# Edge counts in a long one-core kernel: eight edge columns to one 16-bit compare, counted at a step of eight

## The reference, cut to what matters

```
src = jnp.concatenate([edge_index[0], loops])
dst = jnp.concatenate([edge_index[1], loops])
...
denom = jax.ops.segment_sum(ee, dst, num_segments=M)
msg = h[src] * alpha[:, :, None]
agg = jax.ops.segment_sum(msg, dst, num_segments=M).reshape(M, HEADS * NUM_EXPERTS) + b_gat
```

## Time and profile before

| | us |
|---|---|
| median of 3 runs | 13,044.54 (13,042.87 to 13,053.62) |
| profiled execution, its own time | 12,933.95 |
| span of the profile | 12,931.9 |
| PE busy in the span | 6,153.1 |
| DVE busy | 4,820.6 |
| POOL busy | 5,593.1 |
| ACT busy | 2,055.4 |
| L203 and L204, DVE, both stages | 2,253.1 |
| L211, PE, both stages | 598.7 |

### The profile page before, as it was taken

How to read it: one execution, slowest core, us unless ns; L and a number is a source line. 1 busy time by engine, 2 the same in 40 slices (tenths; PEclk the granted TensorE clock), 3 DMA queues, 4 the chain that set the end, 5 groups by cost and what they waited for, 6 DMA issues and landing times. The chain is left out here.

```text
span 12931.9 us, 89860 instructions
## 1 busy us (share of the span) xinstructions
PE 6153.1 (48%) x22715; PEld 3706.2 (29%) x22715; DVE 4820.6 (37%) x13519; ACT 2055.4 (16%) x3797; POOL 5593.1 (43%) x5292
## 2 busy tenths in 40 slices
PE   0115888988869967787322222222222222222256
PEld 0114666666647733333100000100001000000134
DVE  9995555555557843232111111111111111111245
ACT  0001333333323300100011111111111111111000
POOL 0000111111110023323577777777777777777421
PEclk9656777777779977777666665666656666565677
DMA  0002000000021121223211111111111111111343
GB/s 13 0 0 92 21 21 21 20 19 19 18 75 59 55 47 34 50 52 35 49 31 34 30 35 33 31 34 30 35 35 29 34 30 35 35 29 33 93 127 118
DMA packets 406892, 514.78 MB, mean 40 GB/s; under 512 B 240693, under 2 KB 327534, under 8 KB 381938
## 3 DMA queue, kind: packets, MB, share of 16 engines
q1 hardware_dynamic: 209266, 260.41, 7.1%
q0 software_dynamic: 164992, 77.85, 5.6%
q10 hardware_dynamic: 32256, 171.98, 3.3%
HBM read 249.78 MB, written 263.86 MB: 40 GB/s over the span
## 5 line engine op out<-in xcount | busy, mean ns | idle before, releaser
L1498 POOL DMA_INDIRECT e_row<-rows_dram,e_idx x4096 | 4371.7, 1067 | 1352.2 <-issue 1336.2
L1444 PE MATMUL e_bank<-e_hid,e_w 128*128 128x512 f32 x1024 | 827.2, 954 | 4363.6 <-ACT e_hid L1474 3266.2
L1444 PEld LDWEIGHTS e_bank<-e_hid,e_w 128*128 128x128 f32 x1024 | 271.9, 288 | 4801.6 <-issue 4798.6
L1531 DVE COPY e_idx<-e_allidx 128x64 int32 x64 | 13.1, 205 | 3764.3 <-DMA e_row<-rows_dram,e_idx 2797.0
L387 POOL COPY a_xc<-a_xp 128x1573 f32<-128x1573 f32 x104 | 166.4, 1604 | 1347.1 <-PE a_bank L440 1181.5
L204 DVE TENSOR_SCALAR a_cnta_hot<-a_cnta_iota,a_cnta_part 128x256 bf16<-128x256 bf16 x2368 | 702.8, 297 | 0.0
L948 POOL DMA_INDIRECT v_dram<-c_td,c_fidx x256 | 251.2, 981 | 1035.3 <-DVE c_td L1073 959.7
L203 DVE TENSOR_SCALAR a_cnta_hot<-a_cnta_iota,a_cnta_part 128x128 bf16<-128x128 bf16 x2368 | 640.2, 270 | 0.0
L396 POOL DMA_INDIRECT xb_dram<-a_so,a_sidx x256 | 251.3, 982 | 882.4 <-DVE a_sidx L661 499.5
L466 PE MATMUL a_bank<-a_taps,a_xt 121*128 121x100 f32 x2704 | 592.9, 361 | 0.0
L1466 ACT ACTIVATE e_y<-e_bank,e_b 128x512 f32<-128x512 f32 x256 | 175.9, 687 | 2618.5 <-remote 1597.7
(11 more groups left out here) (347 smaller groups left out, 11195.4 us busy)
## 6 DMA issues: line engine op xcount, KB each, us to landing
e_row<-rows_dram,e_idx POOLq DMA_INDIRECT x4096
ys_dram<-e_y ACTq DMA_DIRECT2D x64, 1024.0 KB
f_ye<-ys_dram SPq DMA_DIRECT2D x64, 1024.0 KB
res_dram<-e_st ACTq DMA_DIRECT2D x64, 768.0 KB
xb_dram<-a_taps SPq DMA_DIRECT2D x4, 5120.0 KB, 31.1
b_tok<-xb_dram SPq DMA_DIRECT2D x80, 256.0 KB, 2.7
yb_dram<-b_y ACTq DMA_DIRECT2D x80, 256.0 KB, 2.0
x_dram<-a_xs SPq DMA_DIRECT2D x9, 2048.0 KB, 6.3
```

Source lines behind the costliest of these rows:

```text
L1444: mm = nc.tensor.matmul(bank[UPB + n % DNB][:], w2[:, n % NE, f], hid[:, n % 2, f], start=(f == 0), stop=(f == NF1 - 1))
L1498: nc.gpsimd.indirect_dma_start(row[:, s, u], None, rows, bass.IndirectOffsetOnAxis(ap=idx[:, s, u:u + 1], axis=0)).then_inc(gath[s], 16)
```

## The change

`EdgeCount` now works on blocks of 8 columns. `part` is bf16, `iota` is repeated 8 times with the repeats innermost (128 x 256 x 8), and a slot of the ring holds a block, 384 x 8 results with the 8 columns innermost. `make` issues two tensor_tensor compares for each block whose first column lies in the portion, in place of two tensor_scalar compares for each column. The rings hold 2 blocks (16 columns) in the involution and 5 blocks (40 columns) in the experts. `count` still issues one matmul a column, of the same size; it takes its operands out of the block as `[:, 0:P, z]` and `[:, P:, z]`, so neighbouring elements are 8 elements, 16 bytes, apart. PE waits for the ring once a block. The numbers compared are at most 255, which bf16 holds exactly.

```diff
     def __init__(self, nc, sb, sem, dst, counts, psum, columns, portions, tag,
-                 ring=20):
+                 ring=2):
         self.nc, self.dst, self.counts, self.psum, self.C, self.portions = nc, dst, counts, psum, columns, portions
-        self.RING = ring
+        self.RING, self.BLK = ring, 8
+        assert columns % self.BLK == 0
         self.raw = sb(f"{tag}_raw", [P, 2, columns], I32)
-        self.part = sb(f"{tag}_part", [P, 2, columns], F32)
+        self.part = sb(f"{tag}_part", [P, 2, columns], BF16)
         self.iotai = sb(f"{tag}_iotai", [P, NHI], I32)
-        self.iota = sb(f"{tag}_iota", [P, NHI], BF16)
-        self.hot = sb(f"{tag}_hot", [P, self.RING, P + NHI], BF16)
+        self.iota = sb(f"{tag}_iota", [P, NHI, self.BLK], BF16)
+        self.hot = sb(f"{tag}_hot", [P, self.RING, P + NHI, self.BLK], BF16)
...
-        self.nc.vector.tensor_copy(self.iota[:], self.iotai[:]).then_inc(self.made, 1)
+        self.nc.vector.tensor_copy(self.iota[:], self.iotai[:].unsqueeze(2).broadcast_to([P, NHI, self.BLK])
+                                   ).then_inc(self.made, 1)
...
     def make(self, dve, i, k):
 
         for c in self.cols(k):
-            if c >= self.RING:
-                dve.wait_ge(self.counted, self.C * i + (c - self.RING + 1))
-            h = self.hot[:, c % self.RING]
-            self.nc.vector.tensor_scalar(h[:, 0:P], self.iota[:, 0:P], self.part[:, 0, c:c + 1], None, ALU.is_equal)
-            self.nc.vector.tensor_scalar(h[:, P:], self.iota[:], self.part[:, 1, c:c + 1], None,
+            if c % self.BLK:
+                continue
+            blk = c // self.BLK
+            if blk >= self.RING:
+                dve.wait_ge(self.counted, self.C * i + self.BLK * (blk - self.RING + 1))
+            h = self.hot[:, blk % self.RING]
+            low, high = (self.part[:, d, c:c + self.BLK].unsqueeze(1) for d in range(2))
+            self.nc.vector.tensor_tensor(h[:, 0:P], self.iota[:, 0:P], low.broadcast_to([P, P, self.BLK]),
+                                         ALU.is_equal)
+            self.nc.vector.tensor_tensor(h[:, P:], self.iota[:], high.broadcast_to([P, NHI, self.BLK]),
                                          ALU.is_equal).then_inc(self.hot_ready, 1)
 
     def count(self, pe, i, k):
         for c in self.cols(k):
-            pe.wait_ge(self.hot_ready, self.C * i + (c + 1))
-            h = self.hot[:, c % self.RING]
+            blk, z = divmod(c, self.BLK)
+            if z == 0:
+                pe.wait_ge(self.hot_ready, self.C // self.BLK * i + (blk + 1))
+            h = self.hot[:, blk % self.RING, :, z]
             self.nc.tensor.matmul(self.psum, h[:, 0:P], h[:, P:], start=(c == 0),
                                   stop=(c == self.C - 1)).then_inc(self.counted, 1)
...
         hist = EdgeCount(nc, sb, sem, dst[:, B * COUNT0:], counts, bank[7][:, 0:NHI], COUNT1 // turns, TURN, "cntb",
-                         ring=40)
+                         ring=5)
```

## The result

The changed kernel takes 14,702.63 us (14,696.61 to 14,714.44, 4 runs) against 13,044.53 (13,042.87 to 13,053.62, 4 runs): a ratio of 1.1271 with a 95% interval of 1.1251 to 1.129, 12.7% slower, or 1,658 us. The forecast was 14,540 in a range of 13,250 to 14,900: right in sign and mechanism, 163 us short in size. The counts' lines are now L209 and L211 (compares) and L220 (matmul); L440, L466, L746 and L758 of before are L449, L475, L755 and L767.

The account below looks back on a forecast made before the run. PE was taken to bound both stages. Involution +770, experts +610, hidden counts -32 and clock +145 made +1,493 us: 12,934 becomes 14,427, or 14,540 on the runs' median scale, range 13,250 to 14,900.

Parts of the forecast that it names:

- PE bounds both stages and DVE's saving is worth what PE waits: Involution and experts: PE is nearly always busy, so a faster DVE can give back only PE's waits, 70 us.
- the 70 us of waits: PE's waits for one-hot rows: 66.3 us in the eight images and 3.2 us in the experts.
- the 66 us: The images' part of PE's waits for one-hot rows, 66.3 us in eight images, 8.3 us each.
- Compares of 0.70 and 1.23 us: DVE's two compares for 8 columns, at twice the 32-bit rate: 1.9 us a block, hidden behind PE's 3.02 us.
- The rival with DVE at the 32-bit rate: Step free for PE, but DVE's blocks at the 32-bit rate bind in the images: +160 us, 13,205; chance 0.04.
- 1.8 ns for a separate column, 0.46 us a count: PE's count matmuls: each column apart costs 1.8 ns, 0.353 us more a count than 0.107; chance 0.50.
- A gap doubles the read: Rival for PE's counts: 0.227 us each, the clock as now, +404 us, 13,450; chance 0.25.
- The step is free: Rival: PE's counts stay at 0.107 us and the waits go, 12,975 us, 0.5% faster; chance 0.12.
- The stationary load is hidden: PE's weight loads for the counts, 0.174 us by the sort's transposes, hide beneath the 0.46 us matmul before.
- The last counts of an iteration hide behind the token DMA: Experts: last counts fall into PE's 12.6 us wait for tokens; 8 us hidden, 4 times, -32.
- The clock: PE's granted clock may fall during read-limited counts, slowing experts' turns and images' transposes; half of 290 us taken, +145.
- a worked-out 290: The full clock loss: 140 us in the experts' turns and 150 us in the images' transposes.

Follow-up runs that it names:

- experiment 7: The kernel before, unchanged, profiled on a chip of the experiments to compare stages: 12,029.55 us.
- experiments 4 to 6: The changed kernel with other blocks and rings: blocks of 4, 12,460.5 us; 2 (images) and 16 (experts), 12,675.27; 4 and 6, 12,793.08.
- experiments 2 and 3: The changed kernel with one operand at a step of eight, the other side by side (wrong counts): moving alone 13,643.61 us, stationary alone 11,912.78.
- experiment 4: The changed kernel with blocks of 4 columns (a step of 8 bytes), rings of 5 and 10 blocks: 12,460.5 us, ratio 1.0366 to the kernel before.

## Why the prediction was right, and where it was short

- **PE bounds both stages and DVE's saving is worth what PE waits: held.** With the reads side by side the gain was 115 us, where the 70 us of waits were forecast. By the one image taken apart in experiment 7 some 52 of the 66 us lie in the images' stretches; the rest comes after the counts, in part from a higher clock there, which I hadn't priced.
- **Compares of 0.70 and 1.23 us: held,** 0.684 and 1.218 where nothing disturbs them. The rival with DVE at the 32-bit rate falls.
- **1.8 ns for a separate column, 0.46 us a count: held in its number,** 0.457 (0.348 more than 0.109 for 0.353). The reason given was right only in part: what costs 1.79 ns is a 16-byte line (or a distance of 16 bytes and more), not a column. At 16, 20 and 676 bytes each column has a line of its own, so that no row of before could tell the two apart; experiments 4 to 6 do. "A gap doubles the read" falls, though at 8 bytes the result would have looked like it. "The step is free" falls on all steps from 8 bytes up.
- **The stationary load is hidden: held,** 148 ns in the changed kernel (0.174 us bounded from the sort), and shown by experiments 2 and 3.
- **The last counts of an iteration hide behind the token DMA: held.** PE's wait is 3.44, 1.34 and 1.62 us for 12.63, 13.45 and 13.70. Only three of the four iterations have such a start behind them, so it saves 33 us; -32 was forecast, as four times 8.
- **The clock: mis-sized, and the only term that matters in the miss.** Forecast were +145, half of a worked-out 290, because L466 has gaps too and yet the clock was 0.98 around it. Measured: the images' stage grew by 965 us (4691.9 - 1109.4 less 3727.0 - 1109.6), of which reads are 2,368 x 0.348 = 824 and saved waits -66; 207 remain. The experts grew by 704, of which reads are 1,728 x 0.348 = 601 and the hidden counts -33; 136 remain. Together 343, which is what is left over and not a sum of rows. The rows support it. By the pitches of the rows after, 169 transposes cost 18 us an image and 338 matmuls of L475 9 more, 27, near 207/8 = 26; in a turn of the experts L767 is 2.19 or 0.69 us longer and its transposes 0.44, 1.9 on average over these two turns, near 136/80 = 1.7. I had left L475's part out of the 290 and put it in the range only. The halving was the error: L466's gaps and its clock of 0.98 said nothing of counts at 0.457 us. Nor is it enough that the counts between are limited by their reads too: in experiment 4 they are, at 0.229 us, and the clock is 1.00.
- The sum: clock +198, hidden counts -1, price of a read -20, together +177, against the +176 by which the two stages' growth in the profiles (1,669) exceeds the forecast (1,493). The medians differ by 11 us less.

That the clock's loss follows the reads and not the compares is shown: 0.50 with the moving operand at a step, 1.00 without, in the same window of the same stage (experiments 2 and 3). Why it falls stays open. PE was continuously busy with matmuls limited by their reads when it did, in L428's run before and in the counts after, but that alone doesn't bring it down: by the step, a count and the experts' clock were 0.229 us and 1.00 at 8 bytes, 0.343 and 0.80 at 12, 0.457 and 0.74 to 0.81 at 16.

## What to carry to other kernels

Where a layout is changed to make one engine's instructions larger, price the other engine's reads of it. Where PE bounds the stage, count the 16-byte lines that its moving operand touches, here at 1.79 ns each against 0.42 ns a bf16 column at 2.4 GHz (0.107 us for 256). The reads are not the whole price: here the clock took 343 us more, a fifth of the loss. A layout between the two extremes can serve both sides: pairs gave DVE the same large compares and PE nearly its old pitch. And look for the same price in reads that were always there: L466 had paid it in the kernel before, and a turned layout gave 155 us.

## What the runs showed of the hardware

- The moving operand's price by line, for 256 bf16 columns: 0.109 us side by side, 0.113 at 4 bytes, 0.229 at 8, 0.343 at 12, 0.457 at 16, 0.467 at 32. I had expected one price for any gap.
- The price is the same at different granted clocks (0.457 at 0.74 to 0.81, 0.459 at 0.50), but with it the clock is low for its neighbours too: 0.50 in the images at 16 bytes, 0.80 in the experts at 12. At 8 bytes it isn't, 1.00 in both stages.
- The stationary operand at 16 bytes takes 144 ns to load for 98, far from the moving one's factor of four, and hides behind a count of 0.109 us.
- 507 float32 elements written from PSUM at a step of 400 bytes take 1.07 us on ACT where side by side they take 0.59.
